# Feeding the shared expert from the router's transposed tokens, and a full-height last pass in the down projection

## What is computed

```python
h = _layernorm(x)                       # 4096 tokens x 512
logits = h @ router_w + router_b        # 512 x 16
vals, idx = jax.lax.top_k(softmax(logits), 2)
# shared expert: every token
shared = (silu(h @ sw_gate) * (h @ sw_up)) @ sw_down      # F = 704
# routed experts: up to C = 640 tokens each, gathered by idx
expert_outputs = vmap(mlp)(expert_inputs, w_gate, w_up, w_down)
x = x + shared + weighted(expert_outputs)
```

## Time and profile before

| | us |
|---|---|
| median of 3 runs (2002.61 to 2004.77) | 2002.77 |
| the profiled execution | 2008.5 |
| its span, first to last instruction | 2006.8 |

### The profile page before, as it was taken

One profiled execution on the slowest core, in us unless ns is written; L12 is line 12 of the kernel. 1 busy time (PEld: TensorE's weight loads), 2 busy tenths in 40 slices (PEclk: granted clock), 3 DMA queues, 4 the chain that ended last, 5 costly groups with the idle time before them and its releaser, 6 DMA issues.

```text
span 2006.8 us, 28233 instructions
## 1 busy us (share of the span) xinstructions
PE 1973.7 (98%) x10960; PEld 1704.0 (85%) x10960; DVE 812.5 (40%) x1887; ACT 681.9 (34%) x1389; POOL 805.5 (40%) x661
## 2 busy tenths in 40 slices
PE   8999999999999999999999999999999999999997
PEld 5788888888877777777799888998889998899986
DVE  2566667557663322222223333333333333333331
ACT  3344443444433211111333233332333423333221
POOL 2133134214442300001555554555645656556531
PEclk9999999999999999999999999999999999999998
DMA  7020221021133122221444544445544455444522
GB/s 269 1 85 3 83 85 52 34 85 64 58 122 112 29 49 54 51 54 25 110 116 114 127 110 93 130 116 121 117 90 125 122 116 124 92 120 126 116 27 27
DMA packets 94070, 178.28 MB, mean 89 GB/s; under 512 B 14416, under 2 KB 14416, under 8 KB 93680
## 3 DMA queue, kind: packets, MB, share of 16 engines
q1 hardware_dynamic: 68640, 123.36, 19.7%
q0 software_dynamic: 25296, 53.11, 15.0%
HBM read 127.53 MB, written 48.91 MB: 88 GB/s over the span
## 4 chain that ended last, share of the span: by engine, by line
PE 96%; issue 1%; ACT 1%; DMA 1%; DVE 1%; POOL 0%; SPq 0%; ACTq 0%; DVEq 0%; POOLq 0%
PE ps L70 60%; PE ps L1227 23%; PE ps L628 4%; PE ps L1169 3%; PE ps L634 3%; PE ps L771 1%; PE ps L733 1%; PE ps L641 1%; PE ps L654 1%; ACT buffer L1035 0%; DMA buffer<-tokens_normed 0%; DMA buffer<-in_WkT 0%; DVE buffer L1111 0%; DMA buffer<-in_wts 0%; POOL buffer L982 0%
## 5 line engine op out<-in xcount | busy, mean ns | idle before, releaser
L70 PE MATMUL ps<-buffer,buffer 128*128 128x320 f32 (+1 forms) x6816 | 1248.7, 343 | 5.4 <-DVE buffer L529 2.1
L70 PEld LDWEIGHTS ps<-buffer,buffer 128*128 128x128 f32 x6816 | 1101.5, 188 | 109.5 <-issue 9.3
L1227 PE MATMUL ps<-buffer,buffer 128*128 128x512 f32 (+1 forms) x1904 | 488.2, 403 | 1.5 <-DVE buffer L1111 1.5
L982 POOL TENSOR_TENSOR buffer<-buffer,buffer 128x512 fp32r<-128x512 f32 x289 | 385.6, 1495 | 240.2 <-ACT buffer L1035 239.8
L1227 PEld LDWEIGHTS ps<-buffer,buffer 128*128 128x128 f32 (+1 forms) x1904 | 349.6, 188 | 109.0 <-issue 40.2
L1129 DVE TENSOR_TENSOR buffer<-ps,buffer 128x320 f32<-128x320 f32 (+1 forms) x240 | 127.6, 532 | 617.4 <-ACT buffer L1076 589.5
L1076 ACT ACTIVATE buffer<-ps 128x320 f32<-128x320 f32 (+1 forms) x240 | 112.3, 468 | 585.2 <-PE ps L70 545.1
L1035 ACT ACTIVATE buffer<-buffer 128x512 fp32r<-128x512 f32 (+3 forms) x529 | 269.8, 563 | 58.1 <-PE ps L1227 53.4
L1024 POOL DMA_INDIRECT out_tokens<-buffer,slot_index x80 | 125.5, 1569 | 246.1 <-DVE buffer L1153 233.0
L1111 DVE TENSOR_TENSOR buffer<-buffer,buffer 128x320 fp32r<-128x320 f32 (+1 forms) x240 | 178.5, 744 | 11.6 <-ACT buffer L1035 10.5
L1035 ACT ACTIVATE buffer<-ps 128x512 fp32r<-128x512 f32 x112 | 66.4, 594 | 305.5 <-PE ps L1169 305.5
(11 more groups left out here) (101 smaller groups left out, 989.0 us busy)
## 6 DMA issues: line engine op xcount, KB each, us to landing
buffer<-in_wts SPq DMA_DIRECT2D x289, 256.0 KB
buffer<-in_x SPq DMA_DIRECT2D x8, 1024.0 KB, 5.5
buffer<-in_ctxT SPq DMA_DIRECT2D x8, 1024.0 KB, 7.8
tokens_normed<-buffer SPq DMA_DIRECT2D x8, 1024.0 KB, 4.5
out_tokens<-buffer SPq DMA_DIRECT2D x8, 1024.0 KB, 4.3
buffer<-tokens_normed SPq DMA_DIRECT2D x8, 1024.0 KB, 5.9
out_tokens<-buffer POOLq DMA_DIRECT2D x32, 256.0 KB, 4.0
tokens_normed<-buffer POOLq DMA_DIRECT2D x1, 1280.0 KB, 8.8
```

Of the source, the lines that this page charges most:

```text
L70: last = pe.matmul(out, left, right, start=(i == 0), stop=(i == len(todo) - 1))
L982: pool.tensor_tensor(wl[n % RING][:], wraw[n % RAW][:], wh[n % RING][:].bitcast(F32), ALU.subtract).then_inc(s_wl, 1)
L1227: ins = pe.matmul(down_bank[n % 2][:], left, right, start=(c == 0 and i == 0), stop=(c == FC - 1 and i == len(passes) - 1))
```

## The change

There are two edits.

1. **The shared expert's tokens.** A new DRAM tensor `tokens_normed_T` (`YT`) takes the transposed tokens. After `Y2T` SP stores `prob` to it (one DMA of 1 MB for each batch). `load_tokens` now reads from it, already transposed, into `xt`. For the shared groups `transpose_tile` is no longer called (8 x 4 sets of 4 transposes); `x_hi` and `x_lo` read `xt` in SBUF in place of a PSUM bank. New waits: ACT in `SC` waits until the store of the batch before has read `prob`; DVE waits for the last store ahead of the first result tile, which lies over `prob`; `load_tokens` waits for the store and for `s_xl` in place of `s_xT`. The load of batch 1 no longer waits for the router's last products, but comes behind the store of batch 7. The experts still gather and transpose; they count their transposes by `gathered`.
2. **The last pass of a down tile** takes all 128 rows of `hh` and of the low weights, so that it also adds low x low of that chunk. The number of passes stays 17.

```diff
@@ phase1, sync
+            if name == "Y2T":
+                drained(sp, "Y2T", b, NC - 1)
+                sp.dma_start(YT[b].rearrange("(c p) s -> p c s", p=P), prob[:]).then_inc(s_ytout, 16)
@@ phase1, scalar
             if name == "SC":
+                if b >= 1:
+                    act.wait_ge(s_ytout, 16 * b)
@@ phase2, sync
         def load_tokens(g):
             if g >= 2:
-                sp.wait_ge(s_xT, tiles_before[g - 1])
-            sp.dma_start(xn[g % 2][:, 0:NT, :], Y[g * S:(g + 1) * S, :].rearrange("(t p) d -> p t d", p=P))\
-              .then_inc(s_xn[g % 2], 16)
+                sp.wait_ge(s_xl, tiles_before[g - 1])
+            elif g == 1:
+                sp.wait_ge(attn["s_yout"], 16 * B)
+            sp.wait_ge(attn["s_ytout"], 16 * (g + 1))
+            sp.dma_start(xt[g % 2][:], YT[g].rearrange("(c p) s -> p c s", p=P)).then_inc(s_xn[g % 2], 16)
...
-        sp.wait_ge(attn["s_yout"], 16 * B)
         sp.wait_ge(attn["s_base"], NT * B)
-        filled(sp, "L", B - 1)
+        step("Y2T", B - 1)
@@ phase2, scalar
         def x_hi(g, t):
-            n = tiles_before[g] + t
+            cols = slice(t * P, (t + 1) * P)
+            if groups[g][0] == 0:
+                act.wait_ge(s_xn[g % 2], 16 * (g // 2 + 1))
+                copy(xh[:, :, cols], xt[g % 2][:, :, cols]).then_inc(s_xh, 1)
+                return
+            n = gathered[g] + t
@@ phase2, vector
+            if groups[g][0] == 0:
+                src = xt[g % 2][:, :, cols]
+            else:
+                src = x_bank[(gathered[g] + t) % 2][:].rearrange("p (c n) -> p c n", c=NC)
+            dve.tensor_tensor(xl[:, :, cols], src, xh[:, :, cols].bitcast(F32), ALU.subtract).then_inc(s_xl, 1)
...
                 if n == 0:
                     dve.wait_ge(attn["s_out"], 16 * B)
+                    dve.wait_ge(attn["s_ytout"], 16 * B)
@@ phase2, tensor
         for name, b in order:
-            if name == "TOKENS":
-                for t in range(NT):
-                    transpose_tile(0, t)
-            elif name not in ("RAW", "LOAD", "WEIGHTS"):
+            if name not in ("RAW", "LOAD", "WEIGHTS", "TOKENS"):
                 step(name, b)
...
                 if what == "x":
-                    transpose_tile(gx, t)
+                    if groups[gx][0] > 0:
+                        transpose_tile(gx, t)
                     continue
...
+                    passes = [(hh[:, c, cols], wh_c[:]), (hh[:, c, cols], wl_c[:])]
                     if c < FC - 1:
-                        passes = [(hh[:, c, cols], wh_c[:]), (hh[:, c, cols], wl_c[:]), (hl[:, c, cols], wh_c[:])]
-                    else:
-
-                        passes = [(hh[:, c, cols], wh_c[:]), (hh[0:FH, c, cols], wl_c[0:FH])]
+                        passes.append((hl[:, c, cols], wh_c[:]))
```

More of the change, by code:

```diff
@@ L77, in build @@
     Y = nc.dram_tensor("tokens_normed", (N + PAD, D), F32, kind="Internal").ap()
+    YT = nc.dram_tensor("tokens_normed_T", (B, D, S), F32, kind="Internal").ap()
     slots = nc.dram_tensor("slots", (E * CAP, 2), F32, kind="Internal").ap()
@@ L98, in build, with phase1 @@
         }
-        attn = phase1(nc, ctx, a, Y, shared, at)
-        phase2(nc, ctx, a, Y, shared, at, attn)
-def phase1(nc, ctx, a, Y, shared, at):
+        attn = phase1(nc, ctx, a, Y, YT, shared, at)
+        phase2(nc, ctx, a, Y, YT, shared, at, attn)
+def phase1(nc, ctx, a, Y, YT, shared, at):
     out = a["out"]
@@ L208, in phase1 @@
     s_fill = sem("s_fill")
-    s_out, s_yout = sem("s_out"), sem("s_yout")
+    s_out, s_yout, s_ytout = sem("s_out"), sem("s_yout"), sem("s_ytout")
     s_zero, s_pad = sem("s_zero"), sem("s_pad")
@@ L784, in phase1, with phase2 @@
             "filled": filled, "drained": drained, "s_cl": s_cl, "s_krow": s_krow, "s_xb": s_xb, "s_base": s_base,
-            "s_yout": s_yout, "s_out": s_out, "s_scat": s_scat}
-def phase2(nc, ctx, a, Y, shared, at, attn):
+            "s_yout": s_yout, "s_ytout": s_ytout, "s_out": s_out, "s_scat": s_scat}
+def phase2(nc, ctx, a, Y, YT, shared, at, attn):
     out = a["out"]
@@ L811, in phase2 @@
     xn = [at(52, [ET, D]), at(84, [ET, D])]
+    xt = [at(52, [NC, S]), at(84, [NC, S])]
     xh, xl = at(57, [NC, CAP], F32R), at(62, [NC, CAP], F32R)
@@ L834, in phase2 @@
     tiles_before = [sum(tiles_of[:g]) for g in range(NG + 1)]
+    gathered = [sum(tiles for job, _, tiles, _ in groups[:g] if job > 0) for g in range(NG + 1)]
     def cuts(g):
@@ L958, in sync @@
                 filled(sp, "SC", B - 1, NT - 1)
-                sp.wait_ge(attn["s_yout"], 16)
                 load_tokens(0)
@@ L988, in gather @@
         def gather(g):
-            pool.wait_ge(s_xT, tiles_before[g - 1])
+            if g == B or g == B + 1:
+                pool.wait_ge(s_xl, tiles_before[g - 1])
+            else:
+                pool.wait_ge(s_xT, gathered[g - 1])
             for t in range(ET):
@@ L1045, in x_hi @@
         def x_hi(g, t):
-            n = tiles_before[g] + t
+            cols = slice(t * P, (t + 1) * P)
[4 more added lines that the diff above has]
+            n = gathered[g] + t
             act.wait_ge(s_xT, n + 1)
-            copy(xh[:, :, t * P:(t + 1) * P], x_bank[n % 2][:].rearrange("p (c n) -> p c n", c=NC))\
-                .then_inc(s_xh, 1)
+            copy(xh[:, :, cols], x_bank[n % 2][:].rearrange("p (c n) -> p c n", c=NC)).then_inc(s_xh, 1)
         def h_hi(u):
@@ L1097, in x_lo @@
         def x_lo(g, t):
-            n = tiles_before[g] + t
-            dve.wait_ge(s_xh, n + 1)
+            dve.wait_ge(s_xh, tiles_before[g] + t + 1)
             cols = slice(t * P, (t + 1) * P)
-            dve.tensor_tensor(xl[:, :, cols], x_bank[n % 2][:].rearrange("p (c n) -> p c n", c=NC),
-                              xh[:, :, cols].bitcast(F32), ALU.subtract).then_inc(s_xl, 1)
+            if groups[g][0] == 0:
+                src = xt[g % 2][:, :, cols]
+            else:
+                src = x_bank[(gathered[g] + t) % 2][:].rearrange("p (c n) -> p c n", c=NC)
+            dve.tensor_tensor(xl[:, :, cols], src, xh[:, :, cols].bitcast(F32), ALU.subtract).then_inc(s_xl, 1)
         def h_lo(u):
@@ L1158, in transpose_tile @@
         def transpose_tile(g, t):
[L1159 to L1163, removed]
+            n = gathered[g] + t
+            pe.wait_ge(s_xg[g % 2], 16 * ET * ((g - B) // 2 + 1))
             if n >= 2:
-                pe.wait_ge(s_xl, n - 1)
-            elif n == 0:
-                drained(pe, "X", B - 2)
+                pe.wait_ge(s_xl, tiles_before[g] + t - 1)
             for c in range(NC):
```

## The result

The changed kernel takes 1950.84 us (median of 4 runs, 1949.59 to 1951.26); the kernel before took 2003.77 us on the same chip (4 runs, 2002.61 to 2007.31). The ratio is 0.9732, with a 95% interval of 0.9715 to 0.9749: 52.9 us less, with 50.3 to 57.1 us by the interval. The prediction said 1949, between 1942 and 1958, from a gain of 54 us.

A forecast was written before the change was run, and what follows sets the result against it. PE's own stream was taken to bound the kernel. Gains of 22.2 (shared tails), 29.2 (64-row passes) and 2.4 (TOKENS) make 53.8, say 54 us; 2008.5 − 54 = 1954.5, less the profile offset 1949 us, range 1942 to 1958.

The forecast's parts named there:

- The 64-row pass: Down tiles outside shared tails: weight loads lie bare on both sides, 0.34 to 0.385 us each, 29.2 us together.
- the end-of-tile rival: Down tiles: cost sits at tile end (bank change, semaphore, first write), not the 64 rows; 14 us gain, 1989; chance 5%.
- a rule against the change: Weight loads: time goes by columns, fewer rows take as long, so by it alone full-height last passes would gain nothing.
- The transposes: Down tails on PE: a set of four transposes costs 0.43 us, the rest of 4.69 − 4.25.
- Shared tails: Groups 0 to 6: transposes and 64-row passes both go, 3.23 us a tail, less 0.43 in group 1; 22.2 us.
- TOKENS: Step before `PV`: without 16 transposes `PV` waits only for the last copy of `PT`, 581.26 instead of 583.65; 2.4 us.
- The pitch: Gate and up part of group 3: 132 passes of 512 columns, 0.2275 us each, so 3.87 us a 17-pass tile.
- The cover of the hidden values: Shared tails: DVE's last `h_lo` still comes before PE's 16th pass; margin shrinks from about 0.75 to 0.38 us, cost zero.
- The second rival: Seven shared tails: PE waits for late hidden values, half-clock stretches may follow; up to 15 us back, 1964; chance 8%.
- The new wait in SC: ACT's wait for the transposed-token store, ahead of its first exponential: store lands by 223.7, seven microseconds left; cost zero.
- The third rival: ACT's new wait in `SC` binds if the store lands after 238.4; at 68 GB/s 25 us in seven batches, 2125; chance 2%.
- the offset of the profiled execution: Whole kernel: profiled execution was 5.7 us above the runs' median, perhaps partly half-clock stretches; taken off 1954.5 to give 1949.

The follow-up runs named there:

- The run with the pass inside the tile: Changed kernel with the second pass of the last chunk at 64 rows again, one place earlier, so each down tile ends full-height: 1992.3 us against 2004.03.
- the run with edit 2 alone: Kernel before with only the last pass of all 112 down tiles at 128 rows, shared expert's transposes kept: 1963.59 us against 2004.03, ratio 0.9793.

## Why the prediction was right, step by step

**PE sets the time, and distances between starts are the prices.** Right. The gain was counted with no other engine in the sum, and the count held: 53.8 predicted, 52.9 measured (50.3 to 57.1).

**The 64-row pass.** Right in cause and nearly in size. The run with the pass inside the tile leaves no room for the end-of-tile rival. The idle times of the weight loads (0.35 and 0.25) are the sign of the price and not its size. The size is on PE, in these two rows of the kernel before, which stand around the 752.72 and 753.15 of the earlier trace rows:

```profile
752.40 0.39 PE L1227 MATMUL ps<-buffer,buffer 128*128 128x512 f32 x1
...
753.48 0.39 PE L70 MATMUL ps<-buffer,buffer 128*128 128x512 f32 x1
```

The three distances are 0.32, 0.43 and 0.33 us where the pitch is 0.227: 0.09 + 0.20 + 0.11 = 0.40. What the prediction calls a rule against the change holds for how long a load lasts (183 ns with 64 rows, 189 with 96), but it doesn't give what a pass costs. The terms: an expert tail gave 1.71 us (1.75 predicted), and the run with edit 2 alone gave 40.4 us (39 by the prediction's terms). Taking 0.34 rather than 0.385 where transposes follow was right: a tile of an expert fell by 4.69 − 4.34 = 0.35.

**The transposes.** The price of a set depends on its neighbour: 0.43 us between a 64-row pass and a full one, 0.48 between two full ones (the run with edit 2 alone). In the sum it didn't matter, as both went at once.

**Shared tails.** 18.70 − 15.41 = 3.29 us each (3.23 predicted). Group 1's tail was to give back 0.43; its first wait grew by 0.51.

**TOKENS.** 6.25 − 3.92 = 2.3 us (2.4 predicted). `PV` starts at 580.30 and not at 581.3, since `PT` before it already starts 1.0 us earlier; that is mainly the clock, see below.

**The pitch was mis-sized by a little.** I took 30.03/132 = 0.2275 from the gate part of group 3. The changed kernel does the same 132 passes in 29.93. The missing 0.1 us was a piece of the price itself: the first gate pass came right behind a 64-row pass, and the next start is 0.33 us after it (753.15 to 753.48). Some 2 us over all 22 groups' tails were so left out of the sum. In the prediction's range the lower bounds, 21 + 22 + 2.4, add up to 45.4 and not to 46, which moves nothing.

**The cover of the hidden values** held: PE waits for them only in the tails of groups 1 and 7, as before. In group 2 DVE's last `h_lo` ends with this row:

```profile
726.42 1.46 DVE L1128 TENSOR_TENSOR buffer<-buffer,buffer 128x512 fp32r<-128x512 f32 x2
```

That is 727.88, and the 16th pass comes at 724.86 + 15 × 0.2266 = 728.26: the 0.38 us that the prediction gave as cover. The second rival fell.

**The new wait in SC** doesn't bind. ACT's first exponential is still released by DVE:

```profile
229.84 0.69 ACT L414 ACTIVATE buffer<-ps,nbias 128x512 f32<-128x512 f32 x1 [3.45 <-DVE nbias L553]
```

The third rival's mechanism exists, but it needs over 4 MB more of stores, and then costs PE about a quarter of what ACT waits more (16 of 60 us).

**The offset between profile and median.** The two profiled spans differ by 58.1 us, the medians by 52.9. Most of the 5 us is the clock, which was at its lower level in two more stretches of 3.4 us in the kernel before (1.7 us lost in each). One lies in the stretch from 60 to 120 us, here of the kernel before and then of the changed one (the clock stands ahead of the last two numbers). Both are in the same part of phase 1, where PE gets through ten more matmuls in the changed kernel:

```profile
60.00:120.00 60.00, 57.95 (x317) 48.91 (x316) 31.78 (x88) 26.89 (x49) 13.81 (x12) 0.97 0.00 1
```

```profile
60.00:120.00 60.00, 57.94 (x327) 48.95 (x326) 32.64 (x89) 27.80 (x52) 14.80 (x12) 1.00 0.00 1
```

The other lies at the start of group 8, right behind PE's wait of 1.41 us there, which both kernels have:

```profile
999.60:1003.00 3.40, 3.40 (x14) 3.40 (x14) 0.00 (x0) 2.10 (x5) 3.40 (x4) 0.50 0.85 146
```

```profile
971.60:975.00 3.40, 3.40 (x23) 3.40 (x24) 0.00 (x0) 2.32 (x5) 3.40 (x4) 1.00 0.74 122
```

At both places one execution had a stretch at half clock and the other had none, with the same wait ahead. So subtracting the offset of the profiled execution from the forecast was right. Its size, 5.7 us, was taken against a median of 2002.77; by the four runs' median it is 4.7, so 1 us of the forecast's distance from 1950.84 lies there.

## What to carry to other kernels

Look at the form of every matmul on a busy TensorE: in this kernel one pass of 64 or 32 rows in a stream of 128-row passes cost 0.35 to 0.43 us more than a full pass, the time of one and a half to two full passes, while padding it to 96 or 128 rows cost nothing. If several low passes can't be avoided, put them side by side: two of them cost 0.43 us together, where one cost 0.40. And where a result is transposed for one consumer, storing the transposed form once can spare the same transposes later, if the DMA queues have room and the source buffer stays free long enough. Ask then of every instruction behind the store, on its own queue too, who waits for it.

## What the runs showed of the hardware

- Heights of 64 and 32 rows leave the weight loads bare on both sides (0.35 us ahead, 0.25 behind); 96 rows don't (0.04 ahead). The load's own duration hardly changes (0.18 to 0.19 us).
- The queues moved 408 GB/s in a stretch of 5 us with stores and loads of 1 MB (the run with four more stores), against the 226 GB/s of the first 60 us, which I had taken for a bound.
- Four transposes of 128 x 128 cost 0.48 us between full-height passes of 512 columns, though each lasts 0.27 us in the profile.
- A wait of PE can be followed by a stretch at the lower of the two clock levels, but needn't be: the same 2.1 us wait that ends at about 68 us, and the same 1.4 us wait ahead of group 8, were followed by one of 3.4 us in the profiled execution of the kernel before and not in that of the changed kernel.
